# Additions of 128x768 in three stages of a graph network on Trainium2, each written as eight additions of 128x96

## The reference

```
x = x + L0(relu(layernorm(x)))        # attention over edges
x = x + L1(relu(layernorm(x)))        # gated messages, ends in its own layernorm
x = x + L2(relu(layernorm(x)))        # 16 rounds: h = 0.9 * (A_norm h) + 0.1 * x
x = x + L3(relu(layernorm(x)))        # D^-1/2 (A + I) D^-1/2 (x W) + b
```

## Time and profile before

| What | Value |
|---|---|
| median of 3 executions | 11783.65 us (11783.54 to 11801.92) |
| profiled execution | 11789.84 us, its span 11788.1 us |
| VectorE (DVE) busy | 6249.0 us, 53% of the span, 24009 instructions |
| GpSimd (POOL) busy | 8495.2 us, 72%, 8690 instructions |
| TensorE (PE) busy | 7049.0 us, 60% |
| ScalarE (ACT) busy | 4478.5 us, 38% |
| round one, from VectorE's first to last addition | 2602.3 to 3144.1 us |
| middle rounds, first to last of VectorE's sums (L1945) | 3175.8 to 10183.7 us |
| layer pass, first to last `l_x` addition | 10227.8 to 10736.7 us |
| last pass, first to last `e_o` addition | 10791.0 to 11761.0 us |

### The profile page before, as it was taken

How to read it: one execution, slowest core, us unless ns; L and a number is a source line. 1 busy time by engine, 2 the same in 40 slices (tenths; PEclk the granted TensorE clock), 3 DMA queues, 4 the chain that set the end, 5 groups by cost and what they waited for, 6 DMA issues and landing times. The chain is left out here.

```text
span 11788.1 us, 142166 instructions
## 1 busy us (share of the span) xinstructions
PE 7049.0 (60%) x21306; PEld 4364.2 (37%) x21306; DVE 6249.0 (53%) x24009; ACT 4478.5 (38%) x15400; POOL 8495.2 (72%) x8690
## 2 busy tenths in 40 slices
PE   5688677966655555556555655656555655674222
PEld 4566566654433332333323333333323333343111
DVE  6577897889744444444444444444444444585222
ACT  5699666988622222222222222222222222374221
POOL 6675765747677777777777777777777777776777
PEclk7666667877777877877787777777777777897555
DMA  7998885668754444444444444444444444464222
GB/s 250 305 252 240 274 275 172 215 213 285 232 155 128 118 113 116 117 113 119 113 116 117 113 117 115 115 116 114 117 115 117 113 115 117 143 221 138 70 68 60
DMA packets 970287, 1804.52 MB, mean 153 GB/s; under 512 B 412878, under 2 KB 423548, under 8 KB 970061
## 3 DMA queue, kind: packets, MB, share of 16 engines
q1 hardware_dynamic: 687725, 1384.14, 34.9%
q0 software_dynamic: 282336, 418.19, 17.1%
HBM read 1070.12 MB, written 738.89 MB: 153 GB/s over the span
## 5 line engine op out<-in xcount | busy, mean ns | idle before, releaser
L365 POOL DMA_INDIRECT r_g<-y_t,idx_s x5768 | 5534.5, 960 | 1945.3 <-issue 1842.3
L1945 DVE SCALAR_TENSOR_TENSOR F<-r_g,scan_s,F 128x96 f32<-128x96 f32 x5488 | 1770.4, 323 | 3970.6 <-DMA r_g<-y_t,idx_s 3174.8
L2074 ACT ACTIVATE H<-r_pu,kc_e 128x96 f32 (+1 forms) x5474 | 1340.4, 355 | 5531.9 <-PE r_pu L2046 5497.7
L2046 PE MATMUL r_pu<-r_S,ident 128*128 128x384 f32 x2688 | 1733.3, 793 | 2806.9 <-DVE r_S L1947 2806.9
L2046 PEld LDWEIGHTS r_pu<-r_S,ident 128*128 128x128 f32 x2688 | 677.8, 278 | 3554.9 <-DVE r_S L1947 3221.2
L1947 DVE SCALAR_TENSOR_TENSOR r_S<-r_S,scan_s,r_g 128x96 f32<-128x96 f32 x5488 | 1719.0, 313 | 0.5
L2028 PE MATMUL r_pu<-H,ident 128*128 (+2 forms) x2744 | 1526.4, 648 | 90.3 <-DMA r_c<-c_t 84.6
L2029 PE MATMUL r_pu<-r_c,ident 128*128 128x384 f32 (+1 forms) x2744 | 1338.9, 575 | 0.0
L2028 PEld LDWEIGHTS r_pu<-H,ident 128*128 128x128 f32 x2744 | 774.4, 283 | 759.7 <-issue 645.5
L2029 PEld LDWEIGHTS r_pu<-r_c,ident 128*128 128x128 f32 x2744 | 665.7, 243 | 557.7 <-issue 356.8
L365 POOL DMA_INDIRECT e_kv<-kv_t,idx_s x392 | 417.6, 1065 | 249.0 <-issue 127.4
(11 more groups left out here) (333 smaller groups left out, 12257.5 us busy)
## 6 DMA issues: line engine op xcount, KB each, us to landing
r_c<-c_t SPq DMA_DIRECT2D x686, 384.0 KB, 4.0
y_t<-H SPq DMA_DIRECT2D x672, 384.0 KB, 2.4
r_g<-y_t,idx_s POOLq DMA_INDIRECT x5880
kv_t<-n_kv SPq DMA_DIRECT2D x49, 776.0 KB, 6.7
y_t<-d_yx SPq DMA_DIRECT2D x98, 384.0 KB
agg_t<-e_S SPq DMA_DIRECT2D x49, 416.0 KB, 4.6
x1s_t<-e_xb SPq DMA_DIRECT2D x50, 384.0 KB, 4.6
h_t<-e_h SPq DMA_DIRECT2D x50, 384.0 KB, 5.0
```

The source lines that it names most:

```text
L365: G.indirect_dma_start(out=to(j), out_offset=None, in_=table, in_offset=bass.IndirectOffsetOnAxis(ap=idx_s[:, h, j:j + 1], axis=0)).then_i ...
L1945: own.add(V.scalar_tensor_tensor(out=F[:, 0:D], in0=g[:, j, :], scalar=scan_s[:, h, j, 1:2], in1=F[:, 0:D], op0=ALU.mult, op1=ALU.add))
L2046: last = T.matmul(pu[h % 2][g][:], ident[:], S[:, h % 2, 4 * g:4 * g + 4, :], start=False, stop=True)
L2074: last = A.activation(v[:, j, :], pu[h % 2][j // 4][:, j % 4, :], ACT.Copy, scale=k[:, j, 0:1])
```

## The change

Each addition over a batch in the three stages is written as one addition for each of its eight tiles. Only the last of the eight updates the semaphore. Seven additions of a batch are concerned: four in round one, two in the layer pass, one in the last pass.

```diff
+        def add_by_tile(to, x, y, w=J):
+
+            for j in range(w):
+                last = V.tensor_tensor(to[:, j, :], x[:, j, :], y if len(y.shape) == 2 else y[:, j, :], ALU.add)
+            return last
...
-                        V.tensor_tensor(x3[:, h], xn[:, h], yn[:, h], ALU.add).then_inc(s_x3, 1)
+                        add_by_tile(x3[:, h], xn[:, h], yn[:, h]).then_inc(s_x3, 1)
...
-                        V.tensor_tensor(xo[:, h], x3[:, h], r_all[:, 2:3, :].to_broadcast([P, J, D]), ALU.add
-                                        ).then_inc(s_xo, 1)
+                        add_by_tile(xo[:, h], x3[:, h], r_all[:, 2, :]).then_inc(s_xo, 1)
...
-                        V.tensor_tensor(cy[:, h % 2], cs[:, h], yo[:, h], ALU.add).then_inc(s_cy, 1)
+                        add_by_tile(cy[:, h % 2], cs[:, h], yo[:, h]).then_inc(s_cy, 1)
...
-                        V.tensor_tensor(ot[:, h], zt[:, h], xo[:, h], ALU.add).then_inc(s_o, 1)
+                        add_by_tile(ot[:, h], zt[:, h], xo[:, h]).then_inc(s_o, 1)
...
-                        w = tiles(b, J)
-                        V.tensor_tensor(xb[:, h, 0:w], x3[:, h, 0:w], r_all[:, 2:3, :].to_broadcast([P, w, D]), ALU.add
-                                        ).then_inc(s_xb, 1)
+                        add_by_tile(xb[:, h], x3[:, h], r_all[:, 2, :], tiles(b, J)).then_inc(s_xb, 1)
...
-                            V.tensor_tensor(x3[:, h], xv[:, h % 2], x2[:, h], ALU.add).then_inc(s_x3, 1)
+                            add_by_tile(x3[:, h], xv[:, h % 2], x2[:, h]).then_inc(s_x3, 1)
...
-                        V.tensor_tensor(ot[:, h], so[:, h % 2], x3[:, h], ALU.add).then_inc(s_o, 1)
+                        add_by_tile(ot[:, h], so[:, h % 2], x3[:, h]).then_inc(s_o, 1)
```

## The result

The changed kernel takes 11919.99 us, median of 4 executions (11917.5 to 11923.02), beside 11783.6 us for the kernel before. The ratio is 1.0114, 95% interval [1.0102, 1.0125]: 1.1% slower, +136 us. The forecast was +74 us, 11858, with a range up to 11912. The direction was right; the size was not, and the time lies outside the range.

A forecast was written before the change was run, and what follows sets the result against it. VectorE was taken to bound round one, GpSimd the layer and last passes. Round one +96, layer pass -14 and last pass -8 gave +74 us: 11858 from the median 11783.65 (11864 from the profiled run), range 11825 to 11912.

The forecast's parts named there:

- What bounds each stage: VectorE sets round one's pace, 11.1 us a batch; GpSimd sets that of the layer pass, 10.70, and last pass.
- Rival 3: Round one: GpSimd sets the pace and shorter holds speed it up; -59 us in all, 11725; chance 0.02.
- The price of an addition: VectorE, edited stages: eight small additions overlap and span 1.44 us, +0.49 us for each addition replaced.
- round one's term of 96 us: Round one: four additions a batch, 49 batches, +0.49 us each, nothing covering it: +96 us.
- Rival 1: VectorE, edited stages: no overlap between additions, +1.08 us each; together +241 us, 12025; chance 0.03.
- no longer matter there: Round one: GpSimd's stretched gathers stop mattering, as it has 13.1 us a batch for its 10.1.
- feeding costs (rival 4): Loop passes, 112 more instructions: fetching or dispatching adds a few tenths us a batch, 10 to 40 us; chance 0.05.
- Shorter holds in the layer pass: Layer pass: short additions hold gathers less, batch falls from 10.70 to 10.4 us, 14 us gained; bounds 0 to 20.
- Rival 2: Gathers: holds last through the whole chain of eight; layer pass +38, last pass +14; +148 us, 11932; chance 0.07.
- Last pass: Last pass: addition covered on VectorE, most of the scatters' stretch goes; -8 us, from 0 to -10.6.
- The sum: Whole kernel: 96 - 14 - 8 = +74 us, 11858 from the runs' median; forecast's chance 0.83.

The follow-up runs named there:

- e9: Changed kernel with 80 unawaited semaphore increments in VectorE's program ahead of round one's loop; ratio to the kernel before 1.0076, round one 662.7 us.
- e2: Kernel before with only the layer pass's two additions split into eight; ratio to before 0.9997, layer pass 571.3 us.
- e7: e2 with 220 semaphore increments ahead of the layer pass's loop; ratio to the kernel before 1.002, layer pass 598.9 us.
- e3: Kernel before with only the last pass's one addition split into eight; ratio to before 0.9994, last pass 1016.2 us.
- e6: e4 with 63 semaphore increments more ahead of round one's loop; ratio to the kernel before 1.008, round one 656.4 us.
- e8: e2 with VectorE waiting for its result after each of an addition's first seven parts; ratio to the kernel before 1.0051, layer pass 635.0 us.
- e10: Kernel before with layer-pass additions in two halves, one wait between, and the last pass's addition in eight; 11772.45 us, ratio to before 0.9975.
- e4: Kernel before, long additions kept, with 28 unawaited semaphore increments per batch in round one; ratio to before 1.0043, round one 621.1 us.

## Why the prediction was wrong, by its steps

- **What bounds each stage: right.** VectorE sets round one's pace, GpSimd the layer and last passes. Rival 3 is out: round one grew.
- **The price of an addition: right.** 1.44 us for eight, +0.49 us forecast. e9 measures 93 / (4 x 49) = 0.47, and round one's term of 96 us came out as 93. Rival 1, no overlap, is out. That GpSimd's stretched gathers "no longer matter there" came true with 0.2 us a batch to spare in e9, not 3.
- **The failed step: feeding costs (rival 4).** I read the 0.43 us at the turn and allowed "a few tenths of a microsecond per batch", "10 to 40 us more, 11885 or so", "mostly within my range". The mechanism was named, its size was put at a few tenths a batch, and the sum itself has nothing for it. It is 4 to 6 us per turn or nothing, by where the body lies: 30 us in round one (the changed kernel against e9) and about 27 in the layer pass (598.4 against 571.3 in e2; e7 has it too). In the layer pass the nine gaps are 44.4 us, of which part falls into time in which VectorE would have waited for rows. By stages the forecast was 66 us short (+140 against +74): 57 us are these stalls, 14 the gain that did not come (next point), less 3 and 2 us in the other terms. Nothing in the trace of before could give that price, as no VectorE loop stalls there; then its bound had to be left wider than the rows' 0.43 us. The trace of before does have a VectorE loop, in layer L1, of 327 instructions without a stall, which made the length look harmless; only the place was not.
- **Shorter holds in the layer pass: failed.** I read in the earlier trace rows that a gather gets in between two back-to-back additions, from one at 2859.98 that came in at the border of `d_o` and `r_cy`. For long additions that was right beyond the one: in both engines' timelines of round one before, 33 gathers held by `d_o` and 11 held by `d_xo` all got in at the border with the addition behind it. With chains of short ones it holds in `l_x` and not in `l_xb`, where the gather waits until the chain is over. Rival 2 said so, but took it for every gather and forecast +38 us for the pass. The truth lay between: fewer are held, for longer, the mean stays (1030 against 1031 ns), and the term is 0, not -14 (e2).
- **Last pass: right**, -8 forecast and -9.9 measured (e3 -10.0). The chain of `e_o` lets them in: no scatter takes more than 1172 ns. That it would be a chain of this kind was luck, as nothing in the prediction tells it from `l_xb`.
- **The sum.** 93 + 30 in round one, 27 + 0 in the layer pass, -10 in the last: +140, beside +136 measured; the rest lies in the start and the middle rounds, where nothing was edited. That 11920 is near rival 2's 11932 is chance: it has 52 us for longer holds in the layer and last passes, and what came were the stalls.

Why one chain lets gathers pass and another doesn't is open. A wait between separate steps is not the answer by itself: at the border of `d_xo` and `d_x` all 11 held gathers got in before, and in the changed kernel the gather at 2886.03 did not. No run varied what a chain reads or what stands ahead of it.

## What to carry to other kernels

Eight small instructions in the place of one cost here 0.47 us, 0.07 us for each of the seven more, on an engine that sets the pace, and that is predictable from two rows. What is not is the loop that they stand in: when code is added to a hardware loop, count the body's instructions, compare the instruction queue's packets before and after, and look for idle time without a name at the turn; a few dozen instructions ahead of the loop can remove it (e9) or bring it (e6). To let another engine in on what both need, short instructions suffice in some places and not in others (`l_x` and `l_xb`); a wait between them does in all that ran (e8), and one well placed is cheap (e10).

## What the runs showed of the hardware

- VectorE's loops stalled 4 to 6 us at each turn exactly when their body touched four blocks of 128 instructions, in a fit of nine placements and a forecast of two more (e9). What does the fetching no trace shows. With one such loop the instruction queue moved 40 to 50 packets of 8.2 KB more.
- A gather's issue by GpSimd, 0.94 us alone, ends 0.82 us after the VectorE addition or chain that held it: 1.43 us with one of 768 elements, up to 2.71 us with sixteen of 96 back to back. In e2, 22 of 23 gathers were held to the end of the chain of `l_xb`, and none of 25 to that of `l_x`; with a wait for the result between the parts (e8) none took over 1049 ns.
- Semaphore increments that nobody waits for are not free on VectorE: 28 took 1.1 us in e4.
